# Out product of the last attention batch in two halves; shared expert's down product and two low halves moved to the program's end

## Chip, core and metric

One core of a Trainium2 chip runs the whole program in one launch. The metric is the device time of that launch in microseconds (us). Engines: TensorE (PE, with its weight loads as PEld), VectorE (DVE), ScalarE (ACT), GpSimd (POOL), and SyncE (SP), which here issues DMAs.

## What is computed

Two layers over x (16 batches of 128 rows by 128 columns). Only the first attention and the mixture of experts at the very end are touched:

```
x = x + xattn0(layernorm(x), ctx, ctx, boxes, Wq, Wk, Wv, Wo, ...)   # 16 heads of 64
x = x + ffn0(layernorm(x), ...)                                      # quantised
x = x + mlstm1(layernorm(x), ctx, ctx, ...)
x = x + moe1(layernorm(x), ...)
...
# xattn0, its last line, after softmax(...) @ v for every head
return out @ Wo.T + bo                    # out: 128 rows x (16 heads * 64)
...
# moe1: 16 experts of width 64, two of them picked per row, and a shared expert of width 128
shared_out = silu(x @ shared_gate_w) * (x @ shared_up_w) @ shared_down_w
inter = silu(x_flat @ g) * (x_flat @ u)   # per expert
acc = acc + inter @ d * c[:, None]        # c: the row's coefficient for the expert, mostly 0
return routed.reshape(b, s, h) + shared_out
```

## The kernel before

The program is a row of blocks, one after the other: preparation, the attention loop, the quantised feed-forward layer, the mLSTM layer, the experts. Each block gives every engine its own list of instructions, executed in the order written; engines are tied together by semaphores alone, and between two blocks stands a barrier of all engines. There is no scheduler: the order is the order of the code.

**Attention loop.** A slot per batch b (16 of them, B = 16; four units u of four heads each). Units 0 and 1 hold heads 0 to 7, units 2 and 3 heads 8 to 15. For a unit PE computes the scores, ACT the exponentials, DVE `weigh`s them, ACT and POOL split the result into two f16 halves (`gprob_hi`, `low_gprob`), and PE multiplies them with v (`pv`, L910, into the one PSUM bank psV). DVE divides by the row sums (`normalise`, L1139 and L1142) into `att`. When the units of a half (0: units 0 and 1; 1: units 2 and 3) are normalised, PE transposes that half's four chunks (`att_turn`, L918) into a PSUM bank aux0 or aux1, ACT copies it to `attT` (`attT_out`, L1031), and with both halves there `out_proj` (L923) adds up eight f32 chunk products in aux0. DVE's `residual` (L1160 to L1163) adds this to x and takes the row statistics. The loop is skewed: slot b carries units 2 and 3 and the out product of batch b-1. After the last slot the units 2 and 3 of batch 15 are left over, and a tail does them: `pv` of unit 2, `pv` of unit 3, both transposes, one out product, while DVE normalises and at last runs `residual(15)`. ACT loads the table for the next block (L1114) before its two copies of the tail.

**Experts.** Sixteen experts are taken in eight pairs (EC = 8, e = 0 to 7), the rows in four tiles (NT = 4, t = 0 to 3): 32 steps n = 8t + e. For step n PE computes gate and up (`routed`, L2270, banks psEG and psEU, two of each) and the spread coefficients (`coefficients`, L2306), ACT the silu (`gate`, L2153), DVE two products (`prod` L2238, `inter` L2245), ACT the high f16 half (`high`, L2160), POOL the low f16 half as the difference (`low`, L2109), and PE three steps later (LAG = 3) the down product (`routed_down`, L2277: 12 products of 128x128 into psEY). The shared expert's down product of tile t (`shared_down`, also L2277, from `sh_inter2`) opens the accumulation of that tile, ahead of step 8t's down product. `residual(t)` (L2232) adds the finished tile to x, and SP stores it. The buffers of a step are a ring of four; `downs(n)` says how many down products must have ended before a ring place is written again.

Of the kernel before, what the change touches and what calls it, by code (L numbers as in the profile page):

```python
# [718 lines left out]
def attention_loop(nc, T, sb, scope, x_sb, ctxT2, identb, ident, bnst, mv, later, steps,  # L719
# [66 lines left out]
    with nc.Block() as block:  # L786
# [56 lines left out]
        def _(pe):  # L843
# [62 lines left out]
            def pv(par, u):  # L906
                v = psV[:].rearrange("p a m -> p (a m)")
                for j, h in enumerate(heads(u)):
                    for p_part, v_part in ((0, 0), (0, 1), (1, 0)):
                        mm = mm_(v[:, j * (DK + 1):(j + 1) * (DK + 1)], gprob2[:, u % 2, p_part, j],  # L910
                                 vx2[:, par, v_part, h], start=(j == 0 and p_part + v_part == 0),
                                 stop=(j == HG - 1 and p_part == 1), skip_group_check=True)
                mm.then_inc(pv_psum, 1)

            def att_turn(par, half, into):
                for j in range(4):
                    c = 4 * half + j
                    mm = nc.tensor.transpose(aux[into][:, j], att[:, par, 2 * c:2 * c + 2], ident[:])  # L918
                mm.then_inc(attT_psum, 1)

            def out_proj(into):
                for c in range(CH):
                    mm = mm_(aux[into][:, 0], attT[:, c], woT[:, c], start=(c == 0), stop=(c == CH - 1))  # L923
                mm.then_inc(op_psum, 1)

            def wait_pv(b, u):

                pe.wait_ge(v_ready, 2 * b + u // 2 + 1)
                pe.wait_ge(gplo_ready, UN * b + u + 1)
                after(pe, att_ready, UN * b + u)  # L930
# [68 lines left out]
                    out_proj(0)  # L999

            over_batches(nc.tensor, slots)
            for u in (2, 3):
                wait_pv(B - 1, u)
                pv((B - 1) % 2, u)
            pe.wait_ge(att_ready, UN * B)
            pe.wait_ge(x1_ready, B - 1)
            for half in range(2):
                att_turn((B - 1) % 2, half, half)
            pe.wait_ge(attT_ready, 2 * B)
            out_proj(0)  # L1010

        @block.scalar
        def _(act):
# [14 lines left out]
            def attT_out(b, half, frm):  # L1028
                act.wait_ge(attT_psum, 2 * b + half + 1)
                after(act, op_psum, b)  # L1030
                nc.scalar.copy(attT[:, 4 * half:4 * half + 4], aux[frm][:]).then_inc(attT_ready, 1)  # L1031
# [80 lines left out]

            over_batches(nc.scalar, slots)
            nc.scalar.preload_act_table(ACT.Sqrt)  # L1114
            attT_out(B - 1, 0, 0)
            attT_out(B - 1, 1, 1)

        @block.vector
        def _(dve):
# [34 lines left out]
                                aux[half][:].rearrange("p a m -> p (a m)").rearrange("p (h e) -> p h e", e=DK),  # L1154
                                vx2[:, par, 0, 8 * half:8 * half + 8, 0:DK], ALU.subtract).then_inc(v_ready, 1)

            def residual(b):
                dve.wait_ge(op_psum, b + 1)
                dve.wait_ge(x_biased, 4)
                v.tensor_tensor(x_sb[:, b], x_sb[:, b], aux[0][:, 0], ALU.add).then_inc(x1_ready, 1)  # L1160
                dve.wait_ge(x1_ready, b + 1)
                v.bn_stats(bnst[:, b], x_sb[:, b]).then_inc(stat_ready, 1)
                v.tensor_reduce(later["rowmax"][:, b], x_sb[:, b], AX.X, ALU.max).then_inc(max_ready, 1)  # L1163
# [81 lines left out]
                normalise(B - 1, (B - 1) % 2, u)  # L1245
            dve.wait_ge(stat_ready, B - 1)
            aggregate(v, steps["dve"].on(dve), mv, bnst, range(B - 1))
            residual(B - 1)


def quantise_weights(nc, dve, order, later, stage):
# [765 lines left out]
def moe_phase(nc, sb, scope, x_sb, ident, identb, bnst, mv, rstd, steps, later, out):  # L2017
# [60 lines left out]

    def downs(n):

        return (EC + 1) * (n // EC) + n % EC + 2

    def flat(a):
        return a.rearrange("p b d -> p (b d)")
# [1 line left out]
    with nc.Block() as block:  # L2086
# [8 lines left out]
        @block.gpsimd  # L2095
        def _(pool):
            def multiply(t):
                pool.wait_ge(sh_read, t + 1)
                nc.gpsimd.tensor_tensor(sh_inter[:, t], sh_g[:, t], sh_u[:, t], ALU.mult).then_inc(sh_made, 1)

            def shared_low(t):
                pool.wait_ge(sh_hi, t + 1)
                nc.gpsimd.tensor_tensor(sh_inter2[:, t, 1], sh_inter[:, t], sh_inter2[:, t, 0],
                                        ALU.subtract).then_inc(sh_lo, 1)

            def low(n):
                ring = n % RING
                pool.wait_ge(hi_ready, n + 1)
                nc.gpsimd.tensor_tensor(inter2[:, ring, 1], inter[:, ring], inter2[:, ring, 0],  # L2109
                                        ALU.subtract).then_inc(lo_ready, 1)  # L2110

            pool.wait_ge(coef_ready, 1)
            multiply(0)
            shared_low(0)
            for t in range(NT):
                for e in range(EC):
                    low(EC * t + e)
                    if t < NT - 1 and e == SHARED_AT:
                        multiply(t + 1)
                    if t < NT - 1 and e == SHARED_AT + 2:  # L2120
                        shared_low(t + 1)
# [60 lines left out]
        def _(dve):  # L2182
# [46 lines left out]
            def residual(t):  # L2229
                dve.wait_ge(down_done, (EC + 1) * (t + 1))  # L2230
                xs = flat(x_sb[:, TG * t:TG * t + TG])
                v.scalar_tensor_tensor(out=xs, in0=flat(psY[t % 2][:]), scalar=W_UP ** -2, in1=xs,  # L2232
                                       op0=ALU.mult, op1=ALU.add).then_inc(y_ready, 1)

            for n in range(EC * NT):
                t, e = divmod(n, EC)
                dve.wait_ge(g_ready, n + 1)
                v.tensor_tensor(prod[:, n % RING], act_g[:, n % RING], psU[n % BANKS][:],  # L2238
                                ALU.mult).then_inc(prod_ready, 1)
                if t and e == LAG:  # L2240
                    residual(t - 1)
                dve.wait_ge(prod_ready, n + 1)
                dve.wait_ge(c_psum, n + 1)
                after(dve, lo_ready, n - RING + 1)
                v.tensor_tensor(inter[:, n % RING], prod[:, n % RING], psC[n % BANKS][:],  # L2245
                                ALU.mult).then_inc(inter_ready, 1)
            residual(NT - 1)

        @block.tensor
        def _(pe):  # L2250
# [35 lines left out]
            def shared_down(t):  # L2286
                pe.wait_ge(sh_lo, t + 1)
                if t == 0:
                    pe.wait_ge(coefT_ready, NT)
                after(pe, y_ready, t - 1)  # L2290
                down(t, NC - 1, sh_inter2[:, t], True, False)

            def routed(n):
                if n < BANKS:
# [13 lines left out]

            def routed_down(n):
                t, e = divmod(n, EC)  # L2310
                pe.wait_ge(lo_ready, n + 1)
                down(t, e, inter2[:, n % RING], False, e == EC - 1)

            def turn_coefficients(t):
                for j in range(TG):
# [17 lines left out]
            for n in range(EC * NT):  # L2333
                if n >= BANKS:
                    routed(n)
                    coefficients(n)
                if n >= LAG:
                    if (n - LAG) % EC == 0:
                        shared_down((n - LAG) // EC)
                    routed_down(n - LAG)  # L2340
            for n in range(EC * NT - LAG, EC * NT):
                routed_down(n)


# [26 lines left out]
```

## Time and profile before

| what | value |
|---|---|
| three timed runs | 575.91, 576.12, 576.56 us, median 576.12 |
| the profiled execution | 579.59 us, span of its instructions 577.8 us |
| granted PE clock, mean over the span | 0.843 of full speed |
| busy | PE 459.5 us, DVE 416.4, ACT 380.8, POOL 234.3 |
| attention loop's tail, last slot's out product to the next block's first PE instruction | 327.55 to 338.97 us |
| experts, first gate product to the last residual's end | 490.25 to 575.08 us |

All stretches are in us from the span's start. A row of the timeline gives start, duration, engine, line, operation, output and inputs, how many instructions of the kind follow each other, and in brackets how long the engine stood idle before and who ended that. An f32 product is carried out as two PE instructions, so `out_proj` of eight chunks shows as 16. The granted clock is given as a share of full speed: 1.00 is 2.4 GHz, 0.50 is 1.2 GHz.

### The profile page before, as it was taken

To read this page: it belongs to the slowest core of one execution; us is meant where nothing else is said; L and a number is where in the kernel's file an instruction comes from. 1 tells how busy PE (TensorE), PEld (TensorE's weight loads), DVE (VectorE), ACT (ScalarE), POOL (GpSimd) and SP (SyncE) were. 2 spreads that over 40 slices of the span, in tenths; PEclk is the share of its full clock that TensorE was granted. 3 is DMA by queue.
4 is the path that set the end of the run, shared out by engine and by line. 5 is a ranking of instruction groups with operands and counts; after the bars stand their busy time and mean duration, and the time that the engine had idled before them with its cause. 6 is when DMAs were issued, how large, how long until landed. Compare 5 with 4: busy or idle time off the path is not lost. (4 is left out here: it accounts for less than half of the span.)

```text
span 577.8 us, 15055 instructions
## 1 busy us (share of the span) xinstructions
PE 459.5 (80%) x5672; PEld 343.4 (59%) x5685; DVE 416.4 (72%) x1001; ACT 380.8 (66%) x704; POOL 234.3 (41%) x218
## 2 busy tenths in 40 slices
PE   6256789999999999999999876641677704999996
PEld 5245678888888888888888651240344403366664
DVE  7975768788887877888777769873366677766664
ACT  4674577887888788788885448762566713755443
POOL 3730443233242333324233304018499640276654
PEclk9668899999999999999999965665555555899999
DMA  8204200000000000000000024006000000000001
GB/s 215 84 1 107 55 2 2 3 3 0 0 0 0 0 2 3 0 0 0 0 0 2 1 38 76 0 3 122 3 1 1 3 0 1 1 1 20 19 9 30
DMA packets 18988, 11.67 MB, mean 20 GB/s; under 512 B 9789, under 2 KB 16853, under 8 KB 18941
## 3 DMA queue, kind: packets, MB, share of 16 engines
q1 hardware_dynamic: 18348, 10.34, 7.9%
q0 software_dynamic: 528, 0.71, 0.6%
q8 instruction: 30, 0.49, 0.4%
q14 instruction: 18, 0.14, 0.1%
q10 hardware_dynamic: 64, 0.00, 0.0%
HBM read 6.64 MB, written 1.05 MB: 13 GB/s over the span
## 5 line engine op out<-in xcount | busy, mean ns | idle before, releaser
L822 POOL TENSOR_TENSOR gprob<-gprob 128x512 f16<-128x512 f32 x64 | 74.9, 1170 | 140.9 <-ACT gprob L1036 140.7
L1132 DVE SCALAR_TENSOR_TENSOR gprob<-psG,prob 128x512 f32<-128x512 f32 x64 | 44.0, 688 | 20.3 <-ACT prob L1070 13.1
L1036 ACT CAST gprob<-gprob 128x512 f16<-128x512 f32 x64 | 39.6, 619 | 23.7 <-DVE gprob L1132 23.7
L901 PEld LDWEIGHTS psG<-kron,emb 128*128 128x128 f16 x768 | 49.4, 99 | 9.4 <-issue 0.3
L901 PE MATMUL psG<-kron,emb 128*128 128x128 f16 x768 | 54.6, 222 | 0.0
L1125 DVE TENSOR_REDUCE negmax<-psM 128x4 bf16<-128x512 f32 x64 | 43.6, 683 | 12.0 <-PE psM L879 12.0
L2109 POOL TENSOR_TENSOR inter<-inter 128x512 f16<-128x512 f32 x32 | 37.1, 1159 | 25.8 <-ACT inter L2160 25.8
L1849 POOL TENSOR_TENSOR cmat<-cmat 128x512 f16<-128x512 f32 x32 | 39.4, 1253 | 16.0 <-ACT cmat L1923 15.9
L1070 ACT ACTIVATE prob<-psS 128x512 f32<-128x512 f32 x64 | 34.6, 592 | 13.6 <-PE psS L893 13.4
L1948 DVE SCALAR_TENSOR_TENSOR cmat<-psMS,decay 128x512 f32<-128x512 f32 x32 | 20.6, 686 | 31.3 <-ACT decay L1918 31.3
L889 PE MATMUL psS<-qT,kT 64*128 64x128 f32 x512 | 37.2, 284 | 5.7 <-ACT qT L1018 4.1
L1018 ACT ACTIVATE qT<-aux,biasT 128x128 f32<-128x128 f32 x128 | 36.5, 368 | 7.8 <-PE aux L857 7.8
L2153 ACT ACTIVATE act_g<-psEG 128x512 f32<-128x512 f32 x32 | 19.1, 597 | 31.3 <-PE psEU L2270 30.9
L2238 DVE TENSOR_TENSOR prod<-act_g,psEU 128x512 f32<-128x512 f32 x32 | 22.0, 688 | 23.6 <-ACT act_g L2153 23.5
L816 POOL TENSOR_TENSOR emb<-wave,emb 128x512 f16<-128x512 f32 x15 | 17.4, 1159 | 51.9 <-ACT emb L1062 51.9
L889 PEld LDWEIGHTS psS<-qT,kT 64*128 64x128 f32 x512 | 31.3, 187 | 9.7 <-issue 4.0
L923 PE MATMUL aux<-woT,attT 128*128 128x128 f32 x256 | 34.4, 290 | 2.3 <-ACT attT L1031 0.7
L910 PE MATMUL psV<-vx,gprob 128*128 128x65 f16 x768 | 34.2, 194 | 1.2 <-DVE att L1142 1.2
L923 PEld LDWEIGHTS aux<-woT,attT 128*128 128x128 f32 x256 | 31.2, 199 | 5.0 <-DVE kT L1149 4.0
L1149 DVE TENSOR_TENSOR kT<-aux,biasT 128x512 f32<-128x512 f32 x32 | 22.0, 689 | 14.6 <-PE aux L857 14.6
L857 PE MATMUL aux<-xT,wT 128*128 (+1 forms) x384 | 28.4, 223 | 5.2 <-PEq L323 2.7
L1918 ACT ACTIVATE decay<-psMA 128x512 f32<-128x512 f32 x32 | 17.4, 594 | 20.1 <-PE psMA L1874 20.1
(363 smaller groups left out, 1201.1 us busy)
## 6 DMA issues: line engine op xcount, KB each, us to landing
kS<-ctxT SPq DMA_DIRECT2D x24, 64.0 KB, 2.3
qS<-qT SPq DMA_DIRECT2D x16, 64.0 KB, 2.7
out_dram<-x_sb SPq DMA_DIRECT2D x4, 256.0 KB, 2.3
raw<-in_L_xattn_Wq_dram SPq DMA_DIRECT2D x1, 512.0 KB, 10.0
raw<-in_L_xattn_Wk_dram SPq DMA_DIRECT2D x1, 512.0 KB, 6.9
raw<-in_L_xattn_Wv_dram SPq DMA_DIRECT2D x1, 512.0 KB, 6.9
raw<-in_L_xattn_Wo_dram SPq DMA_DIRECT2D x1, 512.0 KB, 6.3
w<-in_L_ffn_w_dram SPq DMA_DIRECT2D x2, 256.0 KB, 3.0
```

The lines of the kernel that those rows point to most:

```text
L822: nc.gpsimd.tensor_tensor(gprob2[:, u % 2, 1], gprob[:, u % 2], gprob2[:, u % 2, 0], ALU.subtract).then_inc(gplo_ready, 1)
L889: mm_(psS[odd][:, j], kT[rows_of(h), par, h // 2], qT[rows_of(h), par, h // 2], start=(j == 0), stop=False, skip_group_check=True)
L901: mm = mm_(psG[:, :, GN * g:GN * g + GN], emb2[:, par, e_part, g], unit(kron2[:, w_part], u), start=False, stop=(g == NG - 1 and e_part == ...
L910: mm = mm_(v[:, j * (DK + 1):(j + 1) * (DK + 1)], gprob2[:, u % 2, p_part, j], vx2[:, par, v_part, h], start=(j == 0 and p_part + v_part = ...
L923: mm = mm_(aux[into][:, 0], attT[:, c], woT[:, c], start=(c == 0), stop=(c == CH - 1))
L1018: ins = nc.scalar.activation(qT[:, par, c], aux[frm][:, j], ACT.Identity, bias=biasT[:, c:c + 1])
L1036: nc.scalar.copy(gprob2[:, u % 2, 0], gprob[:, u % 2]).then_inc(gphi_ready, 1)
L1070: nc.scalar.activation(prob[:, u % 2], psS[u % 2][:], ACT.Exp, scale=DK ** -0.5 / W_UP ** 2).then_inc(prob_ready, 1)
L1125: v.tensor_reduce(negmax[:, u % 2], psM[u % 2][:], AX.X, ALU.max, negate=True).then_inc(negmax_ready, 1)
L1132: v.scalar_tensor_tensor(out=flat(gprob[:, u % 2]), in0=flat(psG[:]), scalar=1e-6 * G_UP, in1=flat(prob[:, u % 2]), op0=ALU.max, op1=ALU.m ...
L1849: nc.gpsimd.tensor_tensor(cmat2[:, b % 2, 1, g], cmat[:, b % 2, g], cmat2[:, b % 2, 0, g], ALU.subtract).then_inc(clo_ready, 1)
L2109: nc.gpsimd.tensor_tensor(inter2[:, ring, 1], inter[:, ring], inter2[:, ring, 0], ALU.subtract).then_inc(lo_ready, 1)
```

## The change

In the attention's tail the first half of batch 15 (units 0 and 1) is transposed right after the out product of batch 14, into aux1; its four chunk products are put between the `pv` of unit 2 and that of unit 3, into the bank psM0, which is free by then. The second half follows with its own transposes (aux0) and its four chunk products into the same accumulation. `residual(15)` reads psM0.

In the experts the last tile's accumulation is opened by step 24's down product; the shared expert's down product of tile 3 stands between the down products of steps 29 and 30. The low halves of steps 30 and 31 are computed by DVE after its last `inter`, no longer by POOL. `downs` is recounted accordingly.

```diff
+            def out_part(bank, chunks):
+                for c in chunks:
+                    mm = mm_(bank[:, 0], attT[:, c], woT[:, c], start=(c == 0), stop=(c == CH - 1))
+                return mm
+
             def out_proj(into):
-                for c in range(CH):
-                    mm = mm_(aux[into][:, 0], attT[:, c], woT[:, c], start=(c == 0), stop=(c == CH - 1))
-                mm.then_inc(op_psum, 1)
+                out_part(aux[into], range(CH)).then_inc(op_psum, 1)
...
             over_batches(nc.tensor, slots)
-            for u in (2, 3):
-                wait_pv(B - 1, u)
-                pv((B - 1) % 2, u)
+            pe.wait_ge(att_ready, UN * (B - 1) + 2)
+            att_turn((B - 1) % 2, 0, 1)
+            wait_pv(B - 1, 2)
+            pv((B - 1) % 2, 2)
+            pe.wait_ge(attT_ready, 2 * B - 1)
+            out_part(psM[0], range(0, CH // 2))
+            wait_pv(B - 1, 3)
+            pv((B - 1) % 2, 3)
+            pe.wait_ge(x1_ready, B - 1)
             pe.wait_ge(att_ready, UN * B)
-            pe.wait_ge(x1_ready, B - 1)
-            for half in range(2):
-                att_turn((B - 1) % 2, half, half)
+            att_turn((B - 1) % 2, 1, 0)
             pe.wait_ge(attT_ready, 2 * B)
-            out_proj(0)
+            out_part(psM[0], range(CH // 2, CH)).then_inc(op_psum, 1)
...
-            attT_out(B - 1, 0, 0)
-            attT_out(B - 1, 1, 1)
+            attT_out(B - 1, 0, 1)
+            attT_out(B - 1, 1, 0)
...
-            residual(B - 1)
+            residual(B - 1, psM[0])
...
     def downs(n):
-        return (EC + 1) * (n // EC) + n % EC + 2
+        t, e = divmod(n, EC)
+        return (EC + 1) * t + e + (2 if t < NT - 1 or e >= EC - 2 else 1)
...
                 for e in range(EC):
-                    low(EC * t + e)
+                    if t < NT - 1 or e < EC - 2:
+                        low(EC * t + e)
...
+            dve.wait_ge(lo_ready, EC * NT - 2)
+            for n in (EC * NT - 2, EC * NT - 1):
+                dve.wait_ge(hi_ready, n + 1)
+                v.tensor_tensor(inter2[:, n % RING, 1], inter[:, n % RING], inter2[:, n % RING, 0],
+                                ALU.subtract).then_inc(lo_ready, 1)
             residual(NT - 1)
...
                 pe.wait_ge(sh_lo, t + 1)
                 if t == 0:
                     pe.wait_ge(coefT_ready, NT)
-                after(pe, y_ready, t - 1)
-                down(t, NC - 1, sh_inter2[:, t], True, False)
+                if t < NT - 1:
+                    after(pe, y_ready, t - 1)
+                down(t, NC - 1, sh_inter2[:, t], t < NT - 1, False)
...
             def routed_down(n):
                 t, e = divmod(n, EC)
+                if e == 0:
+                    after(pe, y_ready, t - 1)
                 pe.wait_ge(lo_ready, n + 1)
-                down(t, e, inter2[:, n % RING], False, e == EC - 1)
+                down(t, e, inter2[:, n % RING], t == NT - 1 and e == 0, e == EC - 1)
...
                 if n >= LAG:
-                    if (n - LAG) % EC == 0:
+                    if (n - LAG) % EC == 0 and n - LAG < EC * (NT - 1):
                         shared_down((n - LAG) // EC)
                     routed_down(n - LAG)
             for n in range(EC * NT - LAG, EC * NT):
+                if n == EC * NT - 2:
+                    shared_down(NT - 1)
                 routed_down(n)
```

PE's list in the attention's tail, after the last slot's out product, before (a row is line, operation, output and inputs, shape, count, and what it waits for):

```order
L910 MATMUL psV<-vx2,gprob2 128x65 [waits att_ready,gplo_ready,v_ready]
L910 MATMUL psV<-vx2,gprob2 128x65 x11
L910 MATMUL psV<-vx2,gprob2 128x65 [waits att_ready,gplo_ready,v_ready]
L910 MATMUL psV<-vx2,gprob2 128x65 x11
L918 MATMUL aux0<-ident,att 128x128 [waits x1_ready,att_ready]
L918 MATMUL aux0<-ident,att 128x128 x3
L918 MATMUL aux1<-ident,att 128x128 x4
L923 MATMUL aux0<-woT,attT 128x128 [waits attT_ready]
L923 MATMUL aux0<-woT,attT 128x128 x7
```

The same stretch now:

```order
L918 MATMUL aux1<-ident,att 128x128 [waits att_ready]
L918 MATMUL aux1<-ident,att 128x128 x3
L910 MATMUL psV<-vx2,gprob2 128x65 [waits att_ready,gplo_ready,v_ready]
L910 MATMUL psV<-vx2,gprob2 128x65 x11
L923 MATMUL psM0<-woT,attT 128x128 [waits attT_ready]
L923 MATMUL psM0<-woT,attT 128x128 x3
L910 MATMUL psV<-vx2,gprob2 128x65 [waits att_ready,gplo_ready,v_ready]
L910 MATMUL psV<-vx2,gprob2 128x65 x11
L918 MATMUL aux0<-ident,att 128x128 [waits att_ready,x1_ready]
L918 MATMUL aux0<-ident,att 128x128 x3
L923 MATMUL psM0<-woT,attT 128x128 [waits attT_ready]
L923 MATMUL psM0<-woT,attT 128x128 x3
```

One group of four transposes went to the front, and half of the out product went between the two `pv`; behind unit 3's normalisation four transposes and four chunk products are left, where eight and eight stood.

PE's list around the shared down product of tile 3 (step 27, first five rows) and at the program's end (last two rows), before:

```order
L2270 MATMUL psEU<-xTe,moe_w 128x512 x3
L2306 MATMUL psEC<-coefT,spread 128x512
L2277 MATMUL psEY<-moe_w,sh_inter 128x128 x12
L2277 MATMUL psEY<-moe_w,inter 128x128 x12
L2270 MATMUL psEG<-xTe,moe_w 128x512 x3
...
L2306 MATMUL psEC<-coefT,spread 128x512
L2277 MATMUL psEY<-moe_w,inter 128x128 x48
```

And the program's end now:

```order
L2284 MATMUL psEU<-xTe,moe_w 128x512 x3
L2321 MATMUL psEC<-coefT,spread 128x512
L2291 MATMUL psEY<-moe_w,inter 128x128 x24
L2291 MATMUL psEY<-moe_w,sh_inter 128x128 x12
L2291 MATMUL psEY<-moe_w,inter 128x128 x24
```

The twelve products of the shared expert moved from step 27 to a place between the last four groups of twelve.

DVE's list at the program's end now (its last `inter`, the two low halves, the residual):

```order
L2254 TENSOR_TENSOR inter<-prod,psEC1 128x512 [waits moe_lo_ready,moe_c_psum,moe_prod_ready]
L2259 TENSOR_TENSOR inter2<-inter,inter2 128x512 [waits moe_hi_ready,moe_lo_ready]
L2259 TENSOR_TENSOR inter2<-inter,inter2 128x512 [waits moe_hi_ready]
L2241 SCALAR_TENSOR_TENSOR x_sb<-psEY1,x_sb 128x512 [waits moe_down_done]
```

The two rows of L2259 are new there; on POOL the last group of `low` has 8 instructions instead of 10.

## Rows read from the trace of the kernel before

**Rows 1.** The page: span, and busy time, share and instructions of each engine.
```profile
span 577.8 us, 15055 instructions
PE 459.5 (80%) x5672; PEld 343.4 (59%) x5685; DVE 416.4 (72%) x1001; ACT 380.8 (66%) x704; POOL 234.3 (41%) x218
```

**Rows 2.** Timeline of the attention's tail.
```profile
327.55 2.03 PE L923 MATMUL aux<-woT,attT 128*128 128x128 f32 x16
328.25 0.42 DVE L1142 TENSOR_TENSOR att<-psV,rsum 128x256 f32<-128x256 f32 x1
328.80 1.28 ACT L1114 ACT_TABLE_LOAD   x1
329.42 0.53 PE L910 MATMUL psV<-vx,gprob 128*128 128x65 f16 x12
330.33 0.17 DVE L1139 RECIPROCAL rsum<-psV 128x4 f32<-128x4 f32 x1
330.54 0.42 DVE L1142 TENSOR_TENSOR att<-psV,rsum 128x256 f32<-128x256 f32 x1
331.11 0.53 PE L910 MATMUL psV<-vx,gprob 128*128 128x65 f16 x12 [1.17 <-DVE att L1142]
332.38 1.09 PE L918 MATMUL aux<-ident,att 128*128 128x128 f32 x8 [0.73 <-DVE att L1142]
333.07 1.07 ACT L1031 COPY attT<-aux 128x512 f32<-128x512 f32 x2 [2.99 <-PE aux L918]
334.20 3.61 PE L923 MATMUL aux<-woT,attT 128*128 128x128 f32 x16 [0.73 <-ACT attT L1031]
337.84 0.29 DVE L1160 TENSOR_TENSOR x_sb<-x_sb,aux 128x128 f32<-128x128 f32 x1 [4.51 <-PE aux L923]
```

**Rows 3.** Timeline of the last slot: a half's four transposes and its copy.
```profile
325.65 0.63 PE L918 MATMUL aux<-ident,att 128*128 128x128 f32 x4
326.79 0.58 ACT L1031 COPY attT<-aux 128x512 f32<-128x512 f32 x1
```

**Rows 4.** Windows: stretch, length, busy time (instructions) of PE, PEld, DVE, ACT, POOL, clock, DMA share, GB/s.
```profile
330.00:334.00 4.00, 1.62 (x20) 1.29 (x20) 2.55 (x21) 1.01 (x3) 0.12 (x1) 1.00 0.03 6
334.40:334.50 0.10, 0.10 (x2) 0.10 (x2) 0.00 (x0) 0.00 (x0) 0.00 (x0) 0.59 0.00 0
334.50:337.80 3.30, 3.30 (x16) 3.01 (x15) 0.00 (x0) 0.00 (x0) 0.00 (x0) 0.50 0.00 0
75.00:78.00 3.00, 1.68 (x28) 1.53 (x25) 2.97 (x6) 2.24 (x5) 2.00 (x2) 1.00 0.00 0
```

**Rows 5.** The chain that ended last, around step 27 and at the end.
```profile
560.31 1.34 PE psEY L2277 x24
567.52 0.67 PE psEY L2277 x12
573.51 0.86 PE psEY L2277 x12
```

**Rows 6.** Timeline of the program's end.
```profile
569.54 1.50 PE L2277 MATMUL psEY<-moe_w,inter 128*128 128x128 f16 x24
570.71 1.16 POOL L2109 TENSOR_TENSOR inter<-inter 128x512 f16<-128x512 f32 x1 [1.02 <-ACT inter L2160]
570.88 0.69 DVE L2245 TENSOR_TENSOR inter<-prod,psEC 128x512 f32<-128x512 f32 x1
571.60 0.62 ACT L2160 CAST inter<-inter 128x512 f16<-128x512 f32 x1 [0.97 <-DVE inter L2245]
572.30 1.16 POOL L2109 TENSOR_TENSOR inter<-inter 128x512 f16<-128x512 f32 x1 [0.43 <-ACT inter L2160]
574.39 0.69 DVE L2232 SCALAR_TENSOR_TENSOR x_sb<-psEY,x_sb 128x512 f32<-128x512 f32 x1 [2.82 <-PE psEY L2277]
```

**Rows 7.** Costliest groups by line: DVE's subtraction of an f16 half.
```profile
L1153 DVE TENSOR_TENSOR vx<-aux,vx 128x512 f16<-128x512 f32 x32 | 21.3, 686 | 0.7 <-ACT vx L1024 0.3
```

**Rows 8.** Windows of the feed-forward layer's end.
```profile
368.00:372.00 4.00, 3.07 (x10) 1.66 (x11) 3.97 (x6) 3.16 (x5) 0.00 (x0) 0.50 0.00 0
372.00:376.00 4.00, 3.14 (x20) 1.90 (x18) 3.90 (x14) 2.70 (x4) 0.00 (x0) 1.00 0.00 0
```

**Rows 9.** The chain that ended last, in the experts' first steps.
```profile
490.25 1.29 PE psEG L2270 x3
496.47 0.69 PE psEG L2270 x3
```

**Rows 10.** Windows: the experts' first steps.
```profile
490.00:494.00 4.00, 4.00 (x20) 1.52 (x17) 3.33 (x9) 2.71 (x4) 0.00 (x0) 0.50 0.02 4
494.00:496.00 2.00, 2.00 (x9) 0.83 (x8) 1.86 (x5) 0.85 (x3) 0.00 (x0) 0.79 0.00 0
```

More of the change, by code:

```diff
@@ L1155, in v_lo, with residual @@
                                 vx2[:, par, 0, 8 * half:8 * half + 8, 0:DK], ALU.subtract).then_inc(v_ready, 1)
-            def residual(b):
+            def residual(b, bank=aux[0]):
                 dve.wait_ge(op_psum, b + 1)
                 dve.wait_ge(x_biased, 4)
-                v.tensor_tensor(x_sb[:, b], x_sb[:, b], aux[0][:, 0], ALU.add).then_inc(x1_ready, 1)
+                v.tensor_tensor(x_sb[:, b], x_sb[:, b], bank[:, 0], ALU.add).then_inc(x1_ready, 1)
                 dve.wait_ge(x1_ready, b + 1)
```

## The prediction, made before the changed kernel ran

> **What bounds the kernel now.** Start with the page [rows 1]: PE is busy 80% of a span of 577.8 us, more than any other engine. That is an average; the change touches two short stretches where PE is not full, so each is read by itself. About 0.2% of this kernel, 1.15 us, is what a measurement can tell from no change.
>
> First stretch: the timeline of the attention's tail [rows 2]. Read it as one chain without branches: `pv` of unit 3 starts at 331.11 when DVE has normalised unit 2 (330.54 + 0.42, and 0.15 to hand over), eight transposes start at 332.38, the two copies at 333.07, the out product at 334.20, the residual at 337.84. Every engine but the one on the chain is idle, so a microsecond cut from it is a microsecond of the program, as the next block begins behind a barrier. The largest link is the out product: 3.61 us here, while the same 16 instructions of the slot before took 2.03. The windows say why [rows 4]: the granted clock falls between 334.4 and 334.5 from 2.4 to 1.2 GHz and is low until 337.8. Before that PE had been busy only 1.62 of 4 us.
>
> Second stretch: the chain that ended last [rows 5], then the timeline of the end [rows 6]. In the experts' steps the chain stays on PE, step after step, so PE is the bound there; the shared down product makes the piece at 560.31 1.34 us long, where a step without it has 0.67 [rows 5]. At the very end PE runs dry: after the down products that start at 569.54 it waits for POOL's low half of step 30 (570.71 to 571.87) and again for that of step 31 (572.30 to 573.46). The latter started when ACT's high half ended (571.60 + 0.62), so the chain is `inter`, `high`, `low`, down product, residual.
>
> **The change, part by part.** *Attention.* The four transposes of the first half now stand where `pv` of unit 2 began, at 329.42; what they need (unit 1 normalised) ended at 328.25 + 0.42 = 328.67 [rows 2], so they wait for nothing and take 0.63 [rows 3], to 330.05. ACT's copy stands behind the table load, which ends at 328.80 + 1.28 = 330.08; with 0.58 for a copy [rows 3] and 0.06 to hand over (in the tail before: 333.07 + 1.07 to 334.20) PE can begin the first half of the out product at about 330.76. Meanwhile `pv` of unit 2 moves back by about 0.55, half of the 1.09 of eight transposes, to 329.97 to 330.50. DVE then starts on it at 330.54 instead of 330.33, so its result comes about 0.2 later and unit 3 could go at 331.32.
>
> The added wait is the point to watch: PE waits for the copy with `pv` of unit 3 queued behind. The first half's eight instructions cost half the distance 327.55 to 329.42, 0.94, so `pv` of unit 3 starts at 330.76 + 0.94 = 331.70 and not at 331.11: 0.59 late. All behind it is late by as much: transposes at 332.97, a first copy (now the only one) 0.69 after that at 333.66, over at 334.24, and the second half of the out product at 334.30 against 334.20. One copy and four transposes less have nearly paid for the delay.
>
> Then the gain: half the product is left. Bounds: 1.02 at 2.4 GHz (half of 2.03) and 1.80 at 1.2 GHz (half of 3.61). I take 1.80, because it is the row of the same product in the same place, and the clock there had fallen at 334.4, just where the second half would start. The end comes at 336.10, the residual at 336.14 instead of 337.84: 1.70 us saved. With 1.02 it is 335.35, and 2.5 saved. The first half lies where the windows show full clock [rows 4] and is taken at that; at 1.2 GHz it would cost some 0.8 more. DVE's aggregates, the bank psM0 (its last reader is long done) and the wait for batch 14's residual cost nothing: that residual's add ends well before 331.
>
> *Experts.* Removing twelve products from step 27 saves 1.34 - 0.67 = 0.67 on a chain that is all PE [rows 5]; they come back while PE waits for step 30's low half, so they cost nothing there. If that gap closed, they would cost their 0.67 again. The last `inter` then starts at 570.88 - 0.67 = 570.21 and ends at 570.90. DVE does step 30's low half next, ACT step 31's high half at the same time (570.93 to 571.55). A low half on DVE has no row. The nearest is DVE's subtraction of an f16 half from an f32 block of the same shape, 0.686 us [rows 7], against 1.16 on POOL [rows 6]; I take 0.69, and 1.16 as the upper bound, with which the two in a row on one engine would give back the whole gain of this part. Step 30's ends at 571.59, step 31's at 572.28. On POOL, shifted by the 0.67, that last one would have ended at 573.46 - 0.67 = 572.79, so 0.51 is saved. Step 30's down product starts at about 571.64, 0.44 later than POOL would have allowed, and its 0.67 ends at 572.31, just as step 31's half arrives: no loss. The wait on POOL's step 29 costs nothing: POOL had been idle for 1.02 when it began step 30 [rows 6]. Sum of this part: 1.18.
>
> *Total:* 1.70 + 1.18 = 2.88 us. Against the profiled execution, that is a span of 574.9 and a time of 576.7 (579.59 before; it stands 3.5 us, 0.6%, above the median of the three timed runs). Carried to the median, 576.12 - 2.88 = **573.2 us**.
>
> **Rivals.** *The second half runs at 2.4 GHz.* For it: with the first half moved forward PE is busy about 0.9 us more in the stretch ahead, and the trace has a stretch with 1.68 of 3 us busy that kept full clock [rows 4]. Against it: the gaps for `normalise` and the copy remain. It gives 2.5 + 1.18 = 3.7 less: 572.4.
>
> *The slow out product is not what the timed runs had.* The profile is one execution. Had the clock fallen a little later in others, the 16 instructions took 2.03 there, the residual came at 336.26, and against 335.35 only 0.9 is left: 0.9 + 1.18 = 2.1, 574.0. The Trainium skill (TensorE: Matmul & The Clock Gate, Part 1, "What's actually happening") says that the activity window is free-running and does not restart with a kernel; by it the fall is not tied to a place in the program, and the sum would be this one in part of the runs. No row here shows two executions.
>
> *No change.* All later blocks begin 1.7 us earlier; the clock's next rises may not. The feed-forward layer's end has 3.14 of 4 us of PE work at 2.4 GHz from 372 on, after 4 us at 1.2 [rows 8]; should the rise stay where it is, 1.7 us of that stretch is done at half speed, up to 1.3 lost. The experts start at 490.25 at 1.2 GHz, where three products take 1.29 instead of about 0.67, and the rise lies near 494.8 [rows 9, 10]; starting 1.7 earlier under the same rise costs half of it, 0.85. Together 2.2 of the 2.9 is given back: 575.4. Against it: the rises follow PE's work, which comes earlier as well.
>
> *Slower, by the same mechanism in full.* The rise at 372 does not come at all (up to 3.14 lost), and the experts' slow stretch of 4.6 us is had a second time (2.3 lost): 5.4 against 2.9, 578.6. It decides from 4.0 us of loss on. For it: the rise at 372 comes after 3.07 busy of 4 [rows 8], not after unbroken work. Against it: both would have to go wrong at once.
>
> **How the numbers follow.** Chances: forecast 0.37, full clock 0.28, fast out product before 0.20, no change 0.10, slower 0.05. The first three are faster by over 1.15 us: 0.85; same 0.10; slower 0.05. The range begins at 571.8, the 2.4 GHz case less 0.6 for hand-overs and a rise in the experts that comes earlier, and ends at 575.4, the no-change case; below and above it I leave about 0.15.
>
> **What would show it.** Right: in the tail an out product of eight instructions before `pv` of unit 3, starting near 330.8; `pv` of unit 3 near 331.7; a second out product near 334.3 of 1.0 to 1.8 us; the next block's first PE instruction about 1.7 us earlier (2.5 at full clock). At the end two DVE subtractions of about 0.69 each, no POOL work in the last 4 us, PE without a gap in the last two down products, and the distance from the experts' last gate product to the residual shorter by 0.5. Wrong: a first half that starts after 331.3 (a late copy), DVE subtractions near 1.16, a loop that does not get the 0.67 although the twelve products are gone, or the clock's rises of the later stages standing late against their work.

## The result, and the profile after

| | before | changed |
|---|---|---|
| median of 11 runs each | 576.92 us (575.35 to 579.84) | 574.13 us (573.22 to 576.27) |
| profiled execution, and its span | 579.59, 577.8 us | 574.13, 572.4 us |
| granted clock, mean | 0.843 | 0.847 |

The ratio is 0.995 with a 95% interval of 0.9928 to 0.9972, that is 1.6 to 4.2 us less. 2.88 were forecast, and 573.2 us as the time. Of the 0.93 between that and 574.13, 0.80 lie in the starting value: 576.12 was the median of the first three runs, 576.92 that of all eleven. Three timed runs of the experiments below, at 698.61 and 774.22 us (kernel before) and 1477.60 (last version), stood far above all others and are in no median and no ratio. The page of the changed kernel, span and busy times:

```profile
span 572.4 us, 15058 instructions
PE 456.8 (80%) x5673; PEld 342.3 (60%) x5685; DVE 418.9 (73%) x1003; ACT 380.7 (67%) x704; POOL 231.4 (40%) x216
```

Against [rows 1] no sum moves by more than 3 us (PE 2.7 less, DVE 2.5 more, POOL 2.9 less): two instructions more on DVE, two less on POOL. The gain is mostly in when things happen. The timeline of the attention's tail after the change (start, duration, engine, line, operation, idle time before):

```profile
325.71 2.03 PE L923 MATMUL aux<-woT,attT 128*128 128x128 f32 x16
326.96 1.28 ACT L1121 ACT_TABLE_LOAD   x1
327.58 0.60 PE L918 MATMUL aux<-ident,att 128*128 128x128 f32 x4
328.01 0.53 PE L910 MATMUL psV<-vx,gprob 128*128 128x65 f16 x12
328.26 0.58 ACT L1038 COPY attT<-aux 128x512 f32<-128x512 f32 x1
328.79 0.42 DVE L1149 TENSOR_TENSOR att<-psV,rsum 128x256 f32<-128x256 f32 x1
328.89 1.16 PE L923 MATMUL psM<-woT,attT 128*128 128x128 f32 x8 [0.35 <-ACT attT L1038]
329.89 0.53 PE L910 MATMUL psV<-vx,gprob 128*128 128x65 f16 x12
331.25 0.63 PE L918 MATMUL aux<-ident,att 128*128 128x128 f32 x4 [0.83 <-DVE att L1149]
331.91 0.59 ACT L1038 COPY attT<-aux 128x512 f32<-128x512 f32 x1 [3.07 <-PE aux L918]
332.55 1.16 PE L923 MATMUL psM<-woT,attT 128*128 128x128 f32 x8 [0.68 <-ACT attT L1038]
333.75 0.29 DVE L1167 TENSOR_TENSOR x_sb<-x_sb,psM 128x128 f32<-128x128 f32 x1 [1.64 <-PE psM L923]
```

Read it against [rows 2] from the out product of the last slot, which both begin with. From there to the residual of batch 15 it was 337.84 - 327.55 = 10.29 us and is 333.75 - 325.71 = 8.04. The second half takes 1.16, as the first does: the clock stays up, as the windows say (stretch, length, busy time of PE, PEld, DVE, ACT, POOL, clock, DMA share, GB/s):

```profile
328.00:332.50 4.50, 2.69 (x38) 2.21 (x36) 2.76 (x22) 1.42 (x3) 0.28 (x1) 1.00 0.01 2
332.50:334.00 1.50, 1.16 (x8) 0.97 (x8) 0.25 (x1) 0.00 (x0) 0.00 (x0) 1.00 0.00 0
336.00:337.00 1.00, 0.41 (x2) 0.41 (x3) 0.93 (x7) 0.95 (x4) 0.00 (x0) 0.51 0.19 11
```

The fall comes at 336.0 only, in the next block. The program's end, to be held against [rows 6]:

```profile
564.63 1.50 PE L2291 MATMUL psEY<-moe_w,inter 128*128 128x128 f16 x24
565.97 0.69 DVE L2254 TENSOR_TENSOR inter<-prod,psEC 128x512 f32<-128x512 f32 x1
565.97 0.83 PE L2291 MATMUL psEY<-moe_w,sh_inter 128*128 128x128 f16 x12
566.57 1.46 DVE L2259 TENSOR_TENSOR inter<-inter 128x512 f16<-128x512 f32 x2
566.69 0.62 ACT L2169 CAST inter<-inter 128x512 f16<-128x512 f32 x1 [0.97 <-DVE inter L2254]
567.31 1.62 PE L2291 MATMUL psEY<-moe_w,inter 128*128 128x128 f16 x24 [0.51 <-DVE inter L2259]
568.97 0.69 DVE L2241 SCALAR_TENSOR_TENSOR x_sb<-psEY,x_sb 128x512 f32<-128x512 f32 x1 [0.94 <-PE psEY L2291]
```

The shared down product fills what was PE's first wait, the two subtractions follow each other on DVE, and the last 24 products run without a gap. Before, the last residual began 574.39 - 569.54 = 4.85 us after step 28's down product; now 568.97 - 564.63 = 4.34.

**Where the time went**, stage by stage, for every trace of this study; the kernels of the lower rows are explained with the experiments. Each number is a difference of two times in a timeline, good to 0.01. Tail: last slot's out product to the residual of batch 15. Feed-forward: its first PE instruction to the mLSTM's first gate product. mLSTM: from there to the experts' first transpose. Experts' start: from there to tile 0's shared down product. End: tile 1's shared down product to the end of the last residual.

| kernel | out product at | tail | feed-forward | mLSTM | experts' start | end |
|---|---|---|---|---|---|---|
| before | 327.55 | 10.29 | 41.69 | 102.22 | 22.92 | 51.17 |
| before, second profile | 325.12 | 10.30 | 41.71 | 102.21 | 22.76 | 51.16 |
| experts' part only | 327.54 | 10.36 | 41.68 | 102.30 | 22.80 | 49.98 |
| attention's part only | 324.61 | 8.03 | 42.26 | 102.38 | 22.01 | 51.16 |
| changed | 325.71 | 8.04 | 42.53 | 102.15 | 22.01 | 49.98 |
| fillers in the old tail | 325.32 | 8.74 | 42.07 | 102.76 | 23.13 | 51.17 |
| first half behind unit 3 | 328.04 | 7.51 | 42.57 | 102.15 | 22.02 | 49.99 |
| low halves on POOL | 327.34 | 8.03 | 42.44 | 102.13 | 22.02 | 50.49 |
| one low half each | 327.56 | 8.03 | 42.43 | 102.31 | 22.01 | 50.05 |
| PE kept busy | 324.79 | 7.51 | 42.56 | 103.04 | 21.00 | 49.98 |
| PE kept busy longer | 325.32 | 7.51 | 42.59 | 102.26 | 21.28 | 49.99 |

The step between experts' start and end is 18.11 or 18.12 in all of them. So the change takes 2.25 off the tail and 1.19 off the end; the feed-forward layer gives 0.84 back, the experts' start brings 0.91. The first column is not the change's: up to there the two kernels run the same instructions, and two executions of one and the same kernel lie 2.43 us apart. The 5.4 us between the two profiled spans hold 1.84 of that, which is why stages are compared here and not spans.

### The profile page after: what moved, and what is told of

Same layout as the page of the kernel before. It is cut to its first block and busy times, and to the rows that moved or that the text cites. A ratio compares the mean times of both kernels' runs of the same rounds, so it can differ in the third digit from the quotient of the medians.

```text
span 572.4 us, 15058 instructions
## 1 busy us (share of the span) xinstructions
PE 456.8 (80%) x5673; PEld 342.3 (60%) x5685; DVE 418.9 (73%) x1003; ACT 380.7 (67%) x704; POOL 231.4 (40%) x216
## 5 line engine op out<-in xcount | busy, mean ns | idle before, releaser
L901 PE MATMUL psG<-kron,emb 128*128 128x128 f16 x768 | 53.3, 219 | 0.0
L2117 POOL TENSOR_TENSOR inter<-inter 128x512 f16<-128x512 f32 x30 | 34.7, 1158 | 23.7 <-ACT inter L2169 23.7
L923 PE MATMUL aux<-woT,attT 128*128 128x128 f32 x240 | 30.8, 281 | 1.6
L923 PEld LDWEIGHTS aux<-woT,attT 128*128 128x128 f32 x240 | 27.9, 191 | 4.0 <-DVE kT L1156 4.0
```

What stands on the lines that cost most here:

```text
L901: mm = mm_(psG[:, :, GN * g:GN * g + GN], emb2[:, par, e_part, g], unit(kron2[:, w_part], u), start=False, stop=(g == NG - 1 and e_part == ...
L923: mm = mm_(bank[:, 0], attT[:, c], woT[:, c], start=(c == 0), stop=(c == CH - 1))
```

## The experiments

**Each part alone.** The diff was taken apart at the border of the two blocks.

In the first kernel the lines of the experts are those of before, in the second those of the attention:

```diff
             over_batches(nc.tensor, slots)
-            for u in (2, 3):
+            pe.wait_ge(att_ready, UN * (B - 1) + 2)
+            att_turn((B - 1) % 2, 0, 1)
...
-            residual(B - 1)
+            residual(B - 1, psM[0])
```
```diff
+                    if t < NT - 1 or e < EC - 2:
+                        low(EC * t + e)
...
             for n in range(EC * NT - LAG, EC * NT):
+                if n == EC * NT - 2:
+                    shared_down(NT - 1)
                 routed_down(n)
```

> Only the attention's part of the change. Theory (each part cuts its own chain, and the parts add): from the start of the last slot's out product to the residual behind batch 15's, 10.3 us before and 8.0 in the changed kernel's profile, it is 8.0 to 8.8 us here, depending on where the clock falls; the program's end stays as before, 569.54 to 574.39 of that trace, 4.85 us from step 28's down product to the last residual; time 1.7 to 2.5 us below before. Rival (the gain came from a clock that rose earlier in the later stages, not from the tail): the tail is short but the time is within 1 us of before.

> Only the experts' part of the change. Theory: the attention's tail is as before, 10.3 us with a slow out product or 8.7 with one at full clock; from the first shared down product at full clock that the chain shows (524.08 before) to the last residual 50.31 us before is 49.13 here, 1.18 less; time about 1.2 us below before, near what a measurement can tell. Rival (the end's gain needs the attention's part): the distance stays at 50.3.

Attention alone: 575.77 us against 576.97, ratio 0.9977 (0.9961 to 0.9993), tail 8.03, end 51.16. Experts alone: 575.83, ratio 0.9984 (0.9966 to 1.0001), tail 10.36, end 49.98. Each stage answers to its own part to a few hundredths, and neither needs the other. The attention's part fell short of the 1.7 to 2.5 us expected: 1.2, with 0.4 to 2.3 in its interval. Its trace does not show why: the stages there sum to 2.4 less than before (2.26 and 0.91 less, 0.57 and 0.16 more), so what the timed runs lost is open. Experts alone is at the border of what can be told from no change, as expected. The end of that kernel agrees with the prediction's sum instruction by instruction; its clock had risen at 494.73, where that of the trace on which the sum was made rose at 494.84:

```profile
570.22 0.69 DVE L2247 TENSOR_TENSOR inter<-prod,psEC 128x512 f32<-128x512 f32 x1
570.94 0.62 ACT L2162 CAST inter<-inter 128x512 f16<-128x512 f32 x1 [0.97 <-DVE inter L2247]
573.22 0.69 DVE L2234 SCALAR_TENSOR_TENSOR x_sb<-psEY,x_sb 128x512 f32<-128x512 f32 x1 [0.94 <-PE psEY L2284]
```

Forecast were 570.21 for the last `inter`, 570.93 for the high half, 573.21 for the residual.

**The kernel before once more**, to see whether its slow out product was an accident of one execution.

> The kernel before, profiled once more, to see what its stages do in another execution. Theory of the prediction (the clock falls in the gaps of the tail): the out product behind them takes about 3.6 us again. Rival of the prediction (the fall is not tied to the place): it takes 2.0 us, and the tail is 8.7 us instead of 10.3. In both cases the stretch from the first shared down product at full clock in the chain to the last residual is 50.3 us.

It took 3.62 us, and the tail 10.30. The timeline of its tail, and the windows ahead of the product and during it:

```profile
325.12 2.03 PE L923 MATMUL aux<-woT,attT 128*128 128x128 f32 x16
331.76 3.62 PE L923 MATMUL aux<-woT,attT 128*128 128x128 f32 x16 [0.72 <-ACT attT L1031]
```
```profile
327.70:331.70 4.00, 1.62 (x20) 1.29 (x20) 2.41 (x21) 1.07 (x2) 0.00 (x0) 1.00 0.02 6
331.70:335.00 3.30, 3.24 (x15) 3.24 (x16) 0.00 (x0) 0.01 (x1) 0.00 (x0) 0.50 0.00 0
```

With the experts-only kernel, whose tail is the old one, that is three traces of the old tail in which the out product ran at 0.50 (3.61, 3.62, 3.68 us), and none in which it did not.

**What of the tail is clock, what is order.** Products nobody reads go into the old tail's gaps, 128x512 bf16 into the bank psM[1].

```diff
             for u in (2, 3):
                 wait_pv(B - 1, u)
                 pv((B - 1) % 2, u)
+                fill(4 if u == 2 else 2)
...
                 att_turn((B - 1) % 2, half, half)
+            fill(2)
             pe.wait_ge(attT_ready, 2 * B)
             out_proj(0)
```

> The kernel before, with eight products nobody reads put into the gaps of the attention's tail (four behind unit 2's product with v, two behind unit 3's, two behind the transposes), so that PE is busy some 1.7 us more ahead of the out product; their sums go to a bank that is no longer read. Theory (the slow out product of the old tail is the clock falling in those gaps, so 1.6 of the 2.25 us by which the changed tail is shorter come from the clock and 0.65 from the order): the out product takes 2.0 to 2.1 us instead of 3.6, the tail is 8.7 us instead of 10.3. Rival (the out product is slow for its own sake, f32 products right after a copy): 3.6 and 10.3 again, with the granted clock at 1.00 all through it. If the clock falls all the same: 3.6 with 0.50.

The tail took 334.06 - 325.32 = 8.74 us, in the old order. PE's timeline:

```profile
325.32 2.03 PE L923 MATMUL aux<-woT,attT 128*128 128x128 f32 x16
327.56 1.02 PE L1004 MATMUL psM<-identb 128*128 128x512 bf16 x4
329.26 0.59 PE L1004 MATMUL psM<-identb 128*128 128x512 bf16 x2
331.08 0.59 PE L1004 MATMUL psM<-identb 128*128 128x512 bf16 x2
331.97 2.05 PE L923 MATMUL aux<-woT,attT 128*128 128x128 f32 x16 [0.29 <-ACT attT L1037]
```
```profile
328.00:332.00 4.00, 3.10 (x28) 1.63 (x26) 2.32 (x21) 1.07 (x2) 0.00 (x0) 1.00 0.02 6
332.00:334.10 2.10, 2.02 (x16) 1.83 (x16) 0.04 (x1) 0.00 (x0) 0.00 (x0) 1.00 0.00 0
```

PE work that does nothing made the out product 1.56 us faster, with the granted clock at 1.00 throughout. So of the tail's 2.25 us, 1.55 is the clock (10.29 to 8.74) and 0.70 the order (8.74 to 8.04). The theory held, and the rival that the product is slow for its own sake fell. This rests on the trace of one run; that run's time, 576.94 us, tells nothing by itself. In the trace little of the 1.55 us is left at the program's end: the feed-forward layer took 0.38 longer than before, the mLSTM 0.54 (in PE's wait ahead of its first product from `future`, 9.40 us against 8.87; the reason is open) and the experts' start 0.21. From the out product to the end it is 0.4 us less.

**The order of the first half and unit 3.**

```diff
-            pe.wait_ge(attT_ready, 2 * B - 1)
-            out_part(psM[0], range(0, CH // 2))
             wait_pv(B - 1, 3)
             pv((B - 1) % 2, 3)
+            pe.wait_ge(attT_ready, 2 * B - 1)
+            out_part(psM[0], range(0, CH // 2))
```

> The changed kernel with the first half of the out product put behind the product with v of unit 3 instead of ahead of it, so that it runs while DVE normalises unit 3. Theory (the wait for the copy holds up unit 3 by some 0.6 us): unit 3's product starts about 0.4 us earlier after the last slot's out product than in the changed kernel (4.18 there, 3.8 here), the first half then fills PE until about 0.2 us after DVE has finished, and the tail is 0.1 to 0.3 us shorter than 8.04. Rival (the order does not matter, as DVE bounds): 8.04 within 0.05. Rival (the first half now stands in the way of the second transposes): longer than 8.04 by 0.3.

PE's and DVE's timeline of this tail:

```profile
328.04 2.03 PE L923 MATMUL aux<-woT,attT 128*128 128x128 f32 x16
331.70 0.53 PE L910 MATMUL psV<-vx,gprob 128*128 128x65 f16 x12 [0.82 <-DVE att L1149]
332.06 1.13 PE L923 MATMUL psM<-woT,attT 128*128 128x128 f32 x8
332.48 0.42 DVE L1149 TENSOR_TENSOR att<-psV,rsum 128x256 f32<-128x256 f32 x1
333.05 0.63 PE L918 MATMUL aux<-ident,att 128*128 128x128 f32 x4
335.55 0.29 DVE L1167 TENSOR_TENSOR x_sb<-x_sb,psM 128x128 f32<-128x128 f32 x1 [1.64 <-PE psM L923]
```

The tail is 335.55 - 328.04 = 7.51 us, 0.53 shorter, more than the 0.1 to 0.3 expected. Unit 3's product starts 3.66 us after the last slot's out product, against 4.18 in the changed kernel and 3.56 before [rows 2]. And the first half costs nothing that the trace shows where it now stands: it is issued in 0.99 us (332.06 to 333.05) while DVE needs until 332.90, so the transposes wait 0.15, as they do in the changed kernel (DVE done at 330.68 + 0.42 = 331.10, transposes at 331.25). The time is 574.29 us, ratio 0.9944 (0.9924 to 0.9964), against 0.995 of the changed kernel: half a microsecond cannot be told there, in the trace it can.

**The end taken apart.**

First the changed kernel with all of `low` on POOL, then with only the last on DVE:

```diff
-                    if t < NT - 1 or e < EC - 2:
-                        low(EC * t + e)
+                    low(EC * t + e)
...
-            dve.wait_ge(lo_ready, EC * NT - 2)
-            for n in (EC * NT - 2, EC * NT - 1):
-                dve.wait_ge(hi_ready, n + 1)
-                v.tensor_tensor(inter2[:, n % RING, 1], inter[:, n % RING], inter2[:, n % RING, 0],
-                                ALU.subtract).then_inc(lo_ready, 1)
```
```diff
-                    if t < NT - 1 or e < EC - 2:
+                    if t < NT - 1 or e < EC - 1:
                         low(EC * t + e)
...
-            for n in (EC * NT - 2, EC * NT - 1):
+            for n in (EC * NT - 1,):
```

> The changed kernel with both last low halves back on POOL. Theory (the move to DVE is worth 0.51 us by itself, and the shared product 0.67): from the second tile's shared down product to the last residual's end it is 50.5 us, where the changed kernel has 49.98 and the kernel before 51.17. Rival (the shared product's place brings all of it): 50.0.

> The changed kernel with step 30's low half on POOL and only step 31's on DVE. Theory (step 30's half may come 0.4 us later on DVE at no cost, because the chain goes through step 31's high half): the same distance of 49.98 us within 0.1, while step 30's down product starts some 0.4 us earlier. Rival (the two in a row on DVE cost something): shorter by 0.2 to 0.4.

Both on POOL: 50.49 us for the end, so the shared product's place is worth 0.68 (51.17 to 50.49) and DVE 0.51 (to 49.98), as in the sum. One each: 50.05, within the 0.1. Each of the two ran once (576.17 and 576.13 us), so only the traces speak. The last rows of these two show why the middle case gains nothing. First both on POOL:

```profile
568.21 0.62 ACT L2168 CAST inter<-inter 128x512 f16<-128x512 f32 x1 [0.97 <-DVE inter L2253]
568.54 0.84 PE L2285 MATMUL psEY<-moe_w,inter 128*128 128x128 f16 x12 [0.21 <-POOL inter L2117]
568.91 1.16 POOL L2117 TENSOR_TENSOR inter<-inter 128x512 f16<-128x512 f32 x1 [0.43 <-ACT inter L2168]
570.12 0.84 PE L2285 MATMUL psEY<-moe_w,inter 128*128 128x128 f16 x12 [0.74 <-POOL inter L2117]
```

and one each:

```profile
568.61 0.62 ACT L2169 CAST inter<-inter 128x512 f16<-128x512 f32 x1 [0.97 <-DVE inter L2254]
568.93 0.84 PE L2291 MATMUL psEY<-moe_w,inter 128*128 128x128 f16 x12 [0.21 <-POOL inter L2117]
569.33 0.69 DVE L2259 TENSOR_TENSOR inter<-inter 128x512 f16<-128x512 f32 x1 [0.76 <-ACT inter L2169]
570.08 0.84 PE L2291 MATMUL psEY<-moe_w,inter 128*128 128x128 f16 x12 [0.30 <-DVE inter L2259]
```

Step 30's down product starts early in both, 0.33 and 0.32 us behind the start of the last high half, where it is 567.31 - 566.69 = 0.62 in the changed kernel (0.30 earlier; 0.4 was expected). Then PE waits: the last low half is released by the last high half, whatever step 30 did. Only its own length counts, 1.16 or 0.69.

**The clock in the experts.** Products nobody reads keep PE busy between the mLSTM's last product and the experts' transposes, on top of the better order of the tail (first half behind unit 3). The counts are 46 and 10, in a second version 54 and 9.

```diff
             values(B - 1)
+            pe.wait_ge(d_ready, G * B)
+            for k in range(46):
+                mm_(psA[k % RING][:], identb[:], future[:].unsqueeze(1).to_broadcast([P, GH, P]), start=True,
+                    stop=True, skip_group_check=True)
...
             mm_ = nc.tensor.matmul
+            for k in range(10):
+                mm_(psC[1][:], w2[:, 0, 0, 0], w2[:, 0, 0, 0:TG], start=True, stop=True, skip_group_check=True)
             for t in range(NT):
                 wait_normalised(pe, steps, 3, t)
```

> The version with the first half behind unit 3's product, and 56 products nobody reads in PE's idle time of some 17 us between the mLSTM's last product and the experts' first transposes, to keep the clock at 2.4 GHz there. Theory (the clock's late rise in the experts, 2 to 5 us after the first gate product, is what differs between executions there, and it costs up to half of that): from the experts' first transpose to the first tile's shared down product it was 22.9 us before and 22.0 in the changed kernel; here 20.6 to 21.4, and the time 1 to 2 us below the changed kernel's 574.1. Rival (other engines bound these steps): 22.0 within 0.2 although the clock is 1.00 from the first transpose on.

573.05 us, ratio 0.9923 (0.9897 to 0.9948). The experts' start took 21.00 us, where all five kernels with the short tail and no such products have 22.01 or 22.02; the transposes ran faster (first transpose to first gate product 5.94 us, 7.22 or 7.23 in all kernels without them). Behind the first gate product nothing was gained: from it to tile 0's shared down product it took 15.06 us, against 14.78 to 14.80 in the five, as the clock fell at 485.28, 0.31 us after it. And the second group was late and held the first transposes up, so that the mLSTM stage took 103.04; the two stages together are only 0.13 shorter than with the first half behind unit 3 alone (124.04 against 124.17). In brackets, PEq is PE's instruction sequencer, at the barrier between two blocks:

```profile
460.62 12.14 PE L1919 MATMUL psMA<-future,identb 128*128 128x512 bf16 x46
475.36 3.83 PE L2271 MATMUL psEC<-moe_w 128*128 128x512 f16 x10 [2.60 <-PEq L1817]
479.03 1.04 PE L2277 MATMUL psEG<-ident,xn 128*128 128x128 f32 x8
```

> The last version with 54 and 9 such products instead of 46 and 10. In its profile the first group ended 2.6 us before the experts' block began, the clock fell in that gap, and the second group ran at half speed (3.83 us) and held the experts' first transposes up by some 0.9 us. Theory (closing the gap keeps the clock up, and the hold-up goes): from the mLSTM's first gate product to the experts' first transpose 102.2 to 102.5 us instead of 103.04, from there to the first tile's shared down product at most 21.0, time 0.5 to 1 us below 573.05. Rival (a clock that falls behind the second group, in the gaps between the transposes, as it did at 485.28, is all that matters): 103.0 becomes 102.2, but the stretch behind it grows to 22. If the first group now runs past the block's end, it holds the barrier up and the first distance grows instead.

```profile
461.25 13.84 PE L1919 MATMUL psMA<-future,identb 128*128 128x512 bf16 x54
476.01 2.10 PE L2271 MATMUL psEC<-moe_w 128*128 128x512 f16 x9 [0.91 <-PEq L1817]
478.16 1.65 ACT L1326 ACTIVATE xn<-x_sb,ln_shift,rstd 128x128 f32<-128x128 f32 x4
478.79 1.06 PE L2277 MATMUL psEG<-ident,xn 128*128 128x128 f32 x8 [0.68 <-ACT xn L1326]
479.71 1.04 ACT L2144 CAST xTe<-psEG 128x512 f16<-128x512 f32 x2
```

The gap between the groups is 0.91 us instead of 2.60, the clock stays at 1.00 from 465.39 to 485.87, and the second group takes 2.10 instead of 3.83 us; the mLSTM stage is back at 102.26. The experts' start took 21.28, not the 21.0 at most that was expected. The 0.28 more than in the version before lie ahead of the first gate product (6.22 us from the first transpose, against 5.94): the transposes began sooner, but ACT was still normalising (`xn`, L1326) and began to copy them 0.92 us behind their start, against 0.63 there. The fall of the clock behind the first gate product, at 485.87 here and 485.28 there, is not the difference: from that product on both took 15.06. Together the two stages are 0.50 shorter than in the version before it. The time, 572.82 us, ratio 0.9931 (0.9898 to 0.9963), cannot be told from 573.05. Both medians lie about 1 us below the changed kernel's 574.13; the intervals overlap.

## Why the prediction was right, point by point

**Attention, the added wait: right.** `pv` of unit 3 was to come 0.59 later; measured from the out product, 4.18 against 3.56, it is 0.62. The first half began 328.89 - 325.71 = 3.18 us after the out product (3.21 forecast), the second half's start moved by 0.19 (0.10 forecast).

**Attention, the length of the second half: mis-sized.** "I take 1.80, because it is the row of the same product in the same place" is the term that failed. It took 1.16, the other bound within 0.14. The row was of the same product, but not of the same activity ahead of it: the first half, moved forward, is itself work for PE there (2.69 us busy of 4.5 up to the second half, where it had been 1.62 of 4), and the clock stayed at 1.00 through the tail in all four traces with this order and in the three with the better one. The fillers show that more work for PE in the old gaps does the same with nothing else moved. So the tail gained 2.25 instead of 1.70; the full-clock rival named the mechanism.

**The rival that the timed runs had a fast out product before: not borne out.** It was slow in three traces out of three. The Trainium skill's rule named with it (TensorE: Matmul & The Clock Gate, Part 1, "What's actually happening": the activity window is free-running) was not contradicted, as the clock's changes come at other times in each execution (in the traces of the old tail it falls at 334.42, 334.31 and 331.67). But measured from the last slot's out product, these falls lie within 0.31 us of each other. A possible reason, argued and not tested: the last rise ahead of it came 252.55, 252.64 and 252.86 us before the out product, so the place was not free. In the other eight traces that distance was 252.46 to 252.94 us five times and 269.58 to 270.43 three times, the fillers' among these, and the clock stayed up through the tail in all eight; the old tail without fillers was not seen with the longer distance.

**Experts: right.** 0.67 and 0.51 forecast, 0.68 and 0.51 measured, and the subtraction on DVE 0.688 against 0.69. Step 30's late low half cost nothing, and one half on each engine won nothing.

**What the sum left out.** The no-change rival's mechanism, a clock whose rises do not come along, is real at a smaller size. In the feed-forward layer the rise came 44.41 us after the last slot's out product before (371.96) and 44.45 after it now (370.16): it did not move with PE's work, which came 2.25 earlier. In all eleven traces that distance is 43.59 to 44.50 us, with tails of 7.51 to 10.36. So 7.24 us of the layer lay behind it instead of 8.70 (370.16 to 377.40, against 371.96 to 380.66), and the layer took 0.84 longer, where up to 1.3 was put down for this. Nearly all of it was lost there: the layer's first `xf` transposes (L1586, now L1593) began 31.64 us after its first PE instruction before and 31.69 now (370.61 and 366.56). Over all traces the layer is, by and large, longer the less of it lies behind that rise (9.04 us behind it: 41.71 long; 7.83: 42.26; 7.19: 42.57). In the experts it went the other way: the rise came 2.85 us after the first gate product instead of 4.74 (489.63 against 494.84; the product is at 490.10 in the timeline of before, and the 490.25 of [rows 9] is a piece of the chain), and the start took 0.91 less. That rise came 163.06 to 163.91 us after the last slot's out product in the five kernels with the short tail, and 166.98 to 167.29 in the four with the old order, the fillers' among them. With the tail's 0.55 the sum is 3.6 us from stage to stage in the two traces. That the median moved by 2.79 where 2.88 was forecast is in part luck: terms of either sign, none of them in the sum, and an interval of 1.6 to 4.2.

## What to carry to other kernels

Read a slow matmul group's granted clock before its instruction count: here 1.55 of 2.25 us in the tail came from work that filled the gap ahead of it, and products nobody reads kept the clock up as well, though in their one trace most of that gain was lost again in later stages. In a tail whose engines wait for each other, put the half that can run early behind the last unit's product and not ahead of it, so that it fills the wait it does not cause. A step moved off a chain was worth its length on the chain here (0.68 and 0.51 us, 0.67 and 0.51 by the rows), and a change of half a per cent is seen in stages between fixed instructions, when the whole span varies by as much between two executions.

## What was not expected of the hardware

One kernel's two profiled executions reach the attention's last slot 2.43 us apart (327.55 and 325.12), with the clock's changes in the first 80 us at other places; every stage behind that agrees within 0.2 us. The experts' start does not follow the clock all the way. With the rise 2.04, 2.61 and 2.90 us after the first gate product it took 22.01, 22.02 and 22.02; with 4.41 to 5.25 us it took 22.76 to 23.13. The traces show why: DVE's last `coef` (L2224 before, L2233 in the changed kernel) ends 9.39 or 9.40 us after the first gate product in every trace. In the five kernels with the earlier rise PE waits for it and begins the transposes of `coef` (L2333 in the changed kernel) at 9.50 or 9.51; in the other traces PE is still busy then and begins them at 9.64 to 10.48. So up to 2.90 us of low clock DVE's routing set the pace, and with PE kept busy only the transposes ahead of it gained (1.0 to 1.3 us).
